# Normalising step of the first norm, units 3 to 7: from VectorE at item 4 to Pool at the frame's second weight slot

## What is computed

```python
x = x + tanh(g_xattn[0]) * xattn(_layernorm(x), ctx, ctx, mask, Wq, bq, Wk, bk, Wv, bv, Wo, bo)
x = x + tanh(g_ffn[0])  * ffn(_layernorm(x), Wg, W1, b1, W2, b2)   # top 2 of 8, sigmoid gates, gelu

def _layernorm(x, axis=-1, eps=1e-05):
    m = mean(x); v = var(x)
    return (x - m) / sqrt(v + eps)
```

## Time and profile before

| | us |
|---|---|
| median of 3 runs | 500.06 |
| lowest, highest | 498.24, 500.44 |
| the profiled execution | 498.24 |
| its span, first to last instruction | 496.5 |

### The profile page before, as it was taken

The page is one execution under the profiler, slowest core; times in us unless marked ns, Lnnn a source line. Parts: engine busy times, 40 slices in busy tenths (PEclk is TensorE's granted clock), DMA queues, the critical chain, the costliest instruction groups (busy, mean ns, idle before and its releaser), DMA issues.

```text
span 496.5 us, 11071 instructions
## 1 busy us (share of the span) xinstructions
PE 420.1 (85%) x4040; PEld 324.4 (65%) x4040; DVE 308.9 (62%) x810; ACT 219.5 (44%) x553; POOL 186.8 (38%) x194
## 2 busy tenths in 40 slices
PE   5757868988989879862579999999999999999970
PEld 3523435554555445452279999999999999999960
DVE  4774787969868684588835555555555555565530
ACT  2243853655656556700044444444444444444420
POOL 8862721212222122200032545444445454444331
PEclk9885898999999999955569999999999999999995
DMA  7363443534454354302011223332222233333221
GB/s 214 84 187 103 120 150 98 174 115 135 140 146 124 97 170 134 127 0 50 0 56 34 46 45 48 51 52 50 46 44 44 47 49 50 53 47 47 24 27 17
DMA packets 35145, 40.25 MB, mean 81 GB/s; under 512 B 10431, under 2 KB 29747, under 8 KB 35091
## 3 DMA queue, kind: packets, MB, share of 16 engines
q0 software_dynamic: 12608, 27.48, 24.7%
q1 hardware_dynamic: 19953, 11.17, 8.0%
q10 hardware_dynamic: 2532, 0.89, 0.7%
HBM read 25.87 MB, written 9.50 MB: 71 GB/s over the span
## 4 chain that ended last, share of the span: by engine, by line
PE 66%; DVE 18%; issue 4%; DMA 4%; ACT 4%; ACTq 1%; POOL 1%; SPq 0%; POOLq 0%; DVEq 0%
PE bank L1242 7%; PE bank L1226 7%; PE bank L1227 7%; PE bank L1228 7%; PE bank L1243 6%; PE bank L1244 6%; PE bank L1005 6%; DVE rowmax L706 4%; PE bank L1043 3%; PE bank L1022 3%; PE bank L1152 3%; PE bank L1190 2%; PE bank L1027 2%; PE bank L1241 2%; DMA out_rows<-y_sb,scatter_tab 2%
## 5 line engine op out<-in xcount | busy, mean ns | idle before, releaser
L1226 PE MATMUL bank<-xh,W 128*128 128x128 f16 x624 | 121.7, 221 | 1.0 <-DVE xl L920 1.0
L1227 PE MATMUL bank<-xl,W 128*128 128x128 f16 x624 | 121.7, 221 | 0.0
L1228 PE MATMUL bank<-xh,W 128*128 128x128 f16 x624 | 121.7, 221 | 0.0
L631 ACT ACTIVATE h<-bank,b1T 128x128 f32<-128x128 f32 x312 | 89.1, 369 | 70.3 <-PE bank L1228 68.7
L451 POOL DMA_INDIRECT out_rows<-y_sb,scatter_tab x39 | 63.7, 1635 | 113.5 <-DVE y_sb L937 107.5
L1242 PE MATMUL bank<-W,hh 128*128 x312 | 85.5, 274 | 0.0
L1243 PE MATMUL bank<-W,hh 128*128 x312 | 85.0, 273 | 0.0
L1244 PE MATMUL bank<-W,hl 128*128 x312 | 85.0, 273 | 0.0
L928 DVE CAST hh<-h 128x512 f16<-128x512 f32 x78 | 34.1, 437 | 76.1 <-ACT h L631 76.1
L706 DVE TENSOR_REDUCE rowmax<-bank 128x2 f32<-128x308 f32 x128 | 57.2, 472 | 26.2 <-PE bank L1022 25.3
L1226 PEld LDWEIGHTS bank<-xh,W 128*128 x624 | 61.7, 99 | 4.4 <-DVE xl L920 1.4
(11 more groups left out here) (180 smaller groups left out, 671.5 us busy)
## 6 DMA issues: line engine op xcount, KB each, us to landing
W_stage<-in_L_ffn_W POOLq DMA_DIRECT2D x32, 512.0 KB, 4.2
xn_scratch<-attn SPq DMA_DIRECT2D x8, 256.0 KB, 2.2
qst<-qh SPq DMA_DIRECT2D x60, 32.0 KB, 3.0
X_late<-in_x SPq DMA_DIRECT2D x6, 256.0 KB, 7.3
out_rows<-X_late SPq DMA_DIRECT2D x6, 256.0 KB, 2.5
qst<-ql SPq DMA_DIRECT2D x28, 32.0 KB, 3.0
xg<-xn_scratch,gather_tab POOLq DMA_INDIRECT x39, 3.0
out_rows<-y_sb,scatter_tab POOLq DMA_INDIRECT x39, 3.9
```

Of the source, the lines that this page charges most:

```text
L631: ins = nc.scalar.activation(h32[s % 4][:, m * P:(m + 1) * P], H_BANKS[s % 4][:, m * P:(m + 1) * P], ACT.Gelu_apprx_tanh, scale=1.0 / W_SC ...
L1226: nc.tensor.matmul(dst, wh, xh[t % 3][:, cut], start=(c == 0), stop=False)
L1227: nc.tensor.matmul(dst, wh, xl[t % 3][:, cut], start=False, stop=False)
L1228: ins = nc.tensor.matmul(dst, wl, xh[t % 3][:, cut], start=False, stop=(c == KC - 1))
```

## The change

Units 3 to 7 are normalised on Pool. The two instructions stand in front of the chunk at the second slot of frame u (item 5 in frame 0, item 3 in frames 1 to 4), ahead of first_rstd. They wait for the root of their own unit, which Pool made a frame earlier (for unit 3 ahead of the frames), and for the query product of unit u+2. They report on a semaphore of their own, ln1_pool, for which turn_x and the bias addition now wait from unit 3 on. Vector's item 4 loses the call.

```diff
+                    if i == W_SLOTS[u][1] and u + 3 < U:
+                        v = u + 3
+                        pool.wait_ge(rstd1_made, first_norm_of[v])
+                        pool.wait_ge(q_filled, q_nth["q", v - 1])
+                        for j in range(2):
+                            ins = nc.gpsimd.tensor_scalar(xn[:, j, :], x_unit(v)[:, j, :], mv1[:, 2 * v + j, 0:1], rstd1[:, 2 * v + j:2 * v + j + 1],
+                                                          ALU.subtract, ALU.mult)
+                        ins.then_inc(ln1_pool, 1)
                     if i == W_SLOTS[u][1] and u + 4 < U:
                         first_rstd(u + 2)
...
-                    pool.wait_ge(ln1_done, u + 1)
+                    pool.wait_ge(*((ln1_done, u + 1) if u < 3 else (ln1_pool, u - 2)))
...
-                    if i == 4 and live(u + 3):
-                        layernorm1(u + 3)
...
-                pe.wait_ge(ln1_done, v + 1)
+                pe.wait_ge(*((ln1_done, v + 1) if v < 3 else (ln1_pool, v - 2)))
```

More of the change, by code:

```diff
@@ L189, in build @@
         moments1_made, var1_made, rstd1_made = sem("moments1_made"), sem("var1_made"), sem("rstd1_made")
+        ln1_pool = sem("ln1_pool")
         neg_half_made, v_zeroed = sem("neg_half_made"), sem("v_zeroed")
```

## The result

| | us |
|---|---|
| before, median of 9 runs | 499.34 (498.03 to 501.02) |
| changed, median of 9 runs | 503.38 (500.70 to 504.31) |
| ratio | 1.0066, 95% interval 1.0044 to 1.0088 |
| the changed kernel's profiled execution | 504.31, span 502.6 |

The change makes the kernel slower by 0.66%, some 3.3 us. The ratio is formed over all runs; the two medians by themselves lie 4.0 us apart. 0.4 us had been forecast, and 503.38 lies outside the range (498.7 to 502.2). The execution profiled after is the slowest of its nine and the one before was among the fastest, so 6.1 us lie between the two profiles, of which about half is the spread of single runs.

A forecast was written before the change was run, and what follows sets the result against it. Short turns between Vector and TensorE were taken to set the pace; Vector 0, loads 0, frame 0 0.38 and roots 0 gave +0.4 us on the median 500.06, so 500.4, range 498.7 to 502.2.

The forecast's parts named there:

- Vector's freed time: Frames 0 to 4: taking the 0.65 us normalising pair off Vector only lengthens idle time; worth 0.
- Rival (c): Every frame: Vector is short, so what it sheds comes off, 3.3 us faster, 496.8; chance 0.05.
- Sooner loads, later roots: Pool, attention frames: loads start 0.65 us sooner, roots pushed back over negmax in frames 2 and 3; both worth 0.
- rival (a): Frames 2 and 3: Pool's root holds Vector's negmax, 0.18 + 0.40 on top of 0.38, +0.96, 501.0; chance 0.22.
- The place: Frame 0, the one place without slack: TensorE's transposes wait for Pool's pair, +0.38 us.
- The price of Pool's instruction: Each normalising instruction on Pool takes 0.55 us, 1.1 for the pair, with 0.88 and 1.74 as ends.
- rival (b): Pool's pointer tensor_scalar costs 1.28 us: +1.85 in frame 0, negmax covered in frames 2 to 4, +4.1, 504.1; chance 0.11.
- The wait and nothing behind it: Frame 0: TensorE's transposes start 0.38 us later, and nothing behind gives it back; the sum has this alone.

The follow-up runs named there:

- e3: The changed kernel with unit 3's pair on Pool one weight slot sooner, ahead of the bias addition of unit 1; ratio 0.9982 (0.9959 to 1.0004).
- e12: The same kernel as e3, measured again; ratio 1.0007 (0.9994 to 1.0020).
- e1: The changed kernel with unit 3 normalised on Vector again, units 4 to 7 still on Pool; ratio 1.0017 (0.9992 to 1.0041).
- e5: The kernel before plus Pool's pairs at the five places, written to a spare tile nobody reads; ratio 1.0005 (0.9990 to 1.0020).
- e8: The kernel before with an added test at the end, Pool instructions beside Vector rows; Vector's 0.18 us rows took 0.42 beside Pool's tensor_scalar.
- e2: The changed kernel with only unit 3 normalised on Pool, units 4 to 7 on Vector; ratio 1.0078 (1.0050 to 1.0107).
- e7: The kernel before with 27 Pool instructions added at the end, all else idle; two-pointer, two-operation tensor_scalar of 256 columns took 1.22 us.
- e4: The changed kernel with ten identity transposes on TensorE ahead of its wait for unit 3; ratio 1.0018 (1.0001 to 1.0035).
- e6: The changed kernel with two more Pool instructions of the same kind ahead of unit 3's pair; ratio 1.0138 (1.0118 to 1.0158).
- e9: The changed kernel with five identity transposes on TensorE ahead of its wait for unit 3; ratio 1.0058 (1.0031 to 1.0084).

## Why the prediction was wrong

- **Vector's freed time is worth 0.** Right. Idle time 2.50 us before the row that waits for TensorE, before; e3 and e12 have the whole change without its wait and lie at 0.9982 and 1.0007. Rival (c), 3.3 us faster, is out.
- **Sooner loads, later roots: 0.** Right in time (e1, e5). The overlap of root and negmax that was reckoned with did not come about, since the dearer pair pushed the root behind negmax (106.06 against 105.28 in frame 2). The reason given for the roots held all the same: beside pow Vector runs undisturbed (e8), so rival (a) is out.
- **The place.** Right: frame 0 is the one place without slack, and TensorE's transposes there waited for Pool. In e2 only this pair is moved, and the loss is all there.
- **The price of Pool's instruction.** The step that failed first. It took 0.55 us, with 0.87 as the upper end; the row is 1.22. The bounds were built from a memset's slope, a two-input row's slope and the fixed part of a two-column row, on the thought that one tensor read costs less than two. e7 shows that this form has a slope of its own, 3.33 ns a column against 0.83 and 1.63. No row of before had that form at width, so the ends should have gone to the dearest whole row, 1.28, which is what rival (b) took. With 2.45 the step's own working gives 60.68 + 2.45 + 0.14 = 63.27, or 1.73 us of wait; e2 measured 1.65. The agreement is partly luck: the step took the transposes' old start, 61.54, from the chain, where the timeline has 61.38, by which it would be 1.89; and TensorE's own maximum row came 0.27 us later behind the load in e2 than the step assumed (1.42 against 61.25 - 60.10 = 1.15), which takes the rest back.
- **The wait and nothing behind it.** The second step that failed, and as much. The sum had the wait alone and put what follows from TensorE's idling at nothing, without a word on the clock. The piece is longer by 3.51 us with 1.17 of wait in the changed kernel and 2.43 with 1.65 in e2, while e4, with a longer wait and a working TensorE, has no such rest and is at 1.0018. So, in the profiled executions, 1.2 to 1.7 us of wait and 0.8 to 2.3 us of lower clock make up 2.4 to 3.5 us, beside some 3.3 us that the runs lose.
- **Rival (b)** had the right mechanism and price in frame 0 (+1.85), and a wrong one behind it: it let the pair hold negmax in frames 2 to 4 for 2.2 us more. Negmax stayed at 0.19 to 0.20 us; in e8 such an instruction held single rows of Vector, and those for 0.24 us only. Its 504.1 is near the measured time by luck: 1.85 us of its 4.1 are right, and the 2.2 of the frames behind stand where the clock's part is.

What stays open: why a wait in frame 0 is followed by a longer low stretch in frame 1, and how the lost clock is shared out over runs. Each profile shows one execution; the added low stretch lay at 64 to 67 us and past 81 in the changed kernel and past 80 in e2, and further ones come in frames that the change doesn't touch.

## What to carry to other kernels

An instruction form that the trace doesn't hold on that engine is priced by the dearest whole row near its size, not by slopes of other forms: here the bounds of 0.44 to 0.87 us missed 1.22. Work moved to an idle engine is free only where its consumer has slack in every repetition; four of five repetitions had it, and the fifth, whose slot stands at item 5 and not 3, one item ahead of its consumer, made the whole loss until it stood one slot sooner. A wait of TensorE can cost more than its length, since its clock may stay low for longer behind the idle time; whether it does differs from one execution to the next.

## What the runs showed of the hardware

- Pool's tensor_scalar f32, 256 columns: 1.22 us with two pointers and two operations, 0.85 with one immediate; a copy 0.40; tensor_tensor 0.72.
- With two pointers it holds Vector's short tensor_scalar rows twice for 0.24 us in its 1.25; the 512-column tensor_tensor holds one for 0.92 us of its 1.29, to its end; the pow of two columns holds none.
- Vector's two-tensor row can hold Pool as well: Pool's variance row took 0.90 us in place of 0.23 at 63.85, until Vector's weight row (63.44 to 64.66) ended, and the pair took 3.04 us in e3 and 3.50 in e6 beside such a row, in place of 2.45.
- About 2 us of TensorE idling in frame 0, half of it for ScalarE, were followed by 1.2 GHz for 3.4 us in one execution and not in another (e2, 2.7 us idle from 60 to 66); ten throwaway transposes in the idle time took back 2.4 us (1.0066 to 1.0018).
- Over one and the same piece 3.4 us more at 1.2 GHz went with 0.8 us more time beyond the wait (e2, e9), 6.8 us more with 2.3 to 2.4 (changed kernel, e6).
